# Two transformer layers on one core: set-up, sum and order rewritten, and Q's parts, V's bias and the normalisation shared among three engines

## The chip, the cores and the metric

One core of a Trainium2 chip runs the whole program. Its engines are TensorE (PE, with its weight loads shown apart as PEld), VectorE (DVE), ScalarE (ACT), GpSimd (POOL) and SyncE (SP, which only issues DMAs here). Each runs its own instructions strictly in the order of the program, and they meet at semaphores. The metric is the device time of one execution in microseconds (us).

## The reference

`x` is 2 batches x 512 rows x 128. Two layers follow each other.

```
layer 0:  w = softmax over the batch axis of (cond . x) / sqrt(128);  h = x * w
          x = x + down(silu(gate(h)) * up(h))       gate, up: 128 -> 512, down: 512 -> 128
          (inputs rounded to 8 bits by row, weights to -1, 0, 1)
layer 1a: causal attention, 16 heads of 8, with one image key and value ahead of the 512 words
layer 1b: y = c_proj(attention) ;  full attention, 16 heads of 8, on y ;  out_proj
          x3 = layernorm(y + attention(y))
          moe: 4 groups x 2 experts, 128 -> 256 -> 128, one expert chosen for each row
          x = x + layernorm(x3 + moe(x3))
```

## The kernel before

**Instances.** The attention is computed four times: instances a = 0 and 1 are the causal attention of batch 0 and 1, a = 2 and 3 the full attention of batch 0 and 1. An instance needs Q, K and V (steps `q`, `k`, `v`). Q and K are each split into three bf16 parts that add up to the fp32 value: part 1 by ACT (`Qp[:, 0]`), the rest `qres` and parts 2 and 3 by DVE (lines 936 to 939 for Q, 943 to 946 for K). The parts go to DRAM and come back stacked, nine rows for each of the 8 dimensions of a head, into `Qs` and `Ks` [128, 2, 16, 512] (SP's step `v`, lines 489 to 507). Rows 64 and up of these stacks have to be zero or hold fixed values (shift, mask) before that; POOL zeroes them with memsets of 64x4096 fp32 words (lines 564, 565, 573, 574), and SP writes the fixed rows (lines 468 to 473).

**Scores twice.** For each head and each tile of 128 rows, PE computes the scores (line 1232) and DVE reduces them to a row maximum (step `scores`: line 968 for the causal instances, 972 for the full ones), 64 steps an instance. The maxima, negated (`max`), are transposed (`max_rows`) and sent by SP into two rows of `Qs`. Then PE computes the scores again, transposed and shifted by the maximum (`attend`, line 1255, 32 steps an instance), ACT takes the exponential (line 751) and PE multiplies with V (`values`, line 1273; four rounds of four heads, the result in `ps_pv`). ACT copies it out, PE turns it (`turn_back`), and DVE normalises: it adds the image's share from `Zimg` (line 1003, causal instances only), takes the reciprocal of the denominator (1007) and multiplies (1008). `V` gets its bias from DVE on its way out of `ps_misc` (line 953).

**Sum, norm and experts.** Step `sum` computes c_proj's and out_proj's results into `ps_misc`, twelve matmuls after `o_rows` of the batch's second instance:

```
for t in range(NT):
    o = ps[:, t * D:(t + 1) * D]
    pe.matmul(o, OT[:, a, t * P:(t + 1) * P], Wcp[:, :], start=True, stop=False)
    pe.matmul(o, OT[:, 2 + a, t * P:(t + 1) * P], WsqT[:, 0, :], start=False, stop=False)
    mm = pe.matmul(o, ones[0:1, :], brow[:, 2, :], start=False, stop=True)
```

On DVE the same step is the whole layer norm (lines 791 to 809), with POOL's power between its halves (line 620). Then come router and combine weights, and for each of 8 experts `hidden` (PE line 1342 into `ps_s0` and `ps_s1`; DVE and ACT take the relu) and `y` (PE line 1350 into `ps_misc`; DVE adds it to `acc`, line 1074). Step `out` is the last norm, again in one piece.

**Order.** `MERGE` is a string of 576 letters. Each letter names a chain (of `f` and `g`, the first layer and Q, K, V of batch 0 and 1; `0` to `3`, scores; `A` to `D`, attend; `a` to `d`, values and turning back; and others), and takes its next step. The result, `ORDER`, is gone through by every engine, which issues what it has to do in each step. So where DVE's part of a step stands among DVE's work, and PE's among PE's, comes from the one string. `ps_misc` is one bank that most small jobs pass through one after another, and scores have two banks (`ps_s0`, `ps_s1`), or four where no attend is near. The first layer's buffers and those of the later steps lie in one region, `shared`.

## Time and profile before

| | us |
|---|---|
| median of 3 runs | 382.31 (380.33 to 384.16) |
| the profiled execution | 381.2 |
| its span, first to last instruction | 379.4 |
| PE busy | 307.3 (81%) |
| DVE busy | 261.2 (69%) |
| ACT busy | 171.2 (45%) |
| POOL busy | 42.5 (11%) |

The profiled execution took 1.8 us more than its span. Busy time of PE counts a matmul from its start to its modelled end, and matmuls overlap, so a busy PE need not be at its peak. An operation's share of the time of a stage is read from the start of one to the start of the next.

### The profile page before, as it was taken

The numbers are of one execution on the slowest core, as the hardware profiler recorded it, in microseconds if no ns is written. First come the engines' busy times: TensorE is split into PE (matmuls) and PEld (weight loads), VectorE is DVE, ScalarE is ACT, GpSimd is POOL, SyncE is SP. The second block draws the span as 40 slices with busy tenths as digits, with TensorE's granted clock in tenths as the row PEclk, the third lists the DMA queues.
The fourth block names the chain that finished last, engine by engine and source line by source line (L and its number), as shares of the span: only waits on it lengthen the run. The fifth ranks groups of instructions, "written<-read, shape, count | busy, mean of one in ns | idle before, by whom it ended". The sixth has DMA issues, their size and how long they took to land.

```text
span 379.4 us, 5450 instructions
## 1 busy us (share of the span) xinstructions
PE 307.3 (81%) x1900; PEld 153.9 (41%) x1900; DVE 261.2 (69%) x763; ACT 171.2 (45%) x246; POOL 42.5 (11%) x56
## 2 busy tenths in 40 slices
PE   0251985897898999868999989999999987987980
PEld 0120733253453644433433222343434455655760
DVE  3979457997786887869989878877721135557444
ACT  2664134005455657443678565665777511220210
POOL 9189500000000000000000000002000001001001
PEclk9996566558999999999999999999999999999997
DMA  6101307601670004710006700160000000000001
GB/s 184 46 2 18 46 0 214 146 1 50 177 141 1 3 4 148 184 41 2 2 14 189 168 4 0 29 196 2 2 2 0 0 2 0 3 0 28 2 0 29
DMA packets 14719, 19.69 MB, mean 52 GB/s; under 512 B 2142, under 2 KB 12258, under 8 KB 14116
## 3 DMA queue, kind: packets, MB, share of 16 engines
q1 hardware_dynamic: 14404, 19.06, 19.3%
q0 software_dynamic: 288, 0.28, 0.6%
q8 instruction: 15, 0.25, 0.3%
q14 instruction: 12, 0.10, 0.1%
HBM read 13.99 MB, written 4.72 MB: 49 GB/s over the span
## 4 chain that ended last, share of the span: by engine, by line
PE 48%; DVE 24%; issue 14%; DMA 6%; ACT 5%; POOL 1%; SPq 1%; POOLq 0%; DVEq 0%; ACTq 0%
PE ps_pv L1273 11%; DVE mx L972 8%; PE ps_s L1232 8%; PE ps_t L1255 7%; DMA Qs<-nmT 5%; PE ps_s L1342 4%; PE ps_misc L1350 3%; PE ps_misc L1208 2%; DVE shared L968 1%; DVE shared L809 1%; DVE probs L902 1%; DMA X<-in_x 1%; ACT probs L751 1%; PE ps_misc L1238 1%; DVE mx L968 1%
## 5 line engine op out<-in xcount | busy, mean ns | idle before, releaser
L751 ACT ACTIVATE probs<-ps_t 128x1024 f32<-128x1024 f32 (+2 forms) x128 | 106.6, 862 | 62.9 <-PE ps_t L1258 33.9
L972 DVE TENSOR_REDUCE mx<-ps_s 128x1 f32<-128x512 f32 x128 | 82.0, 686 | 14.2 <-PE ps_s L1232 14.0
L1232 PE MATMUL ps_s<-Ks,Qs 128*128 128x512 bf16 (+3 forms) x237 | 78.0, 353 | 9.5 <-DVE mx L972 3.0
L1255 PE MATMUL ps_t<-Qs,Ks 128*128 128x512 bf16 (+3 forms) x256 | 67.9, 340 | 5.2 <-DMA Qs<-nmT 5.1
L1273 PE MATMUL ps_pv<-probs,Vs 128*32 128x512 f32 (+3 forms) x512 | 57.2, 524 | 0.4 <-ACT probs L751 0.2
L968 DVE CUSTOM_DVE_ANT_0 shared<-ps_s,shared 128x256 bf16<-128x256 f32 (+3 forms) x109 | 47.3, 465 | 10.9 <-PE ps_s L1232 10.3
L1232 PEld LDWEIGHTS ps_s<-Ks,Qs 128*128 128x128 bf16 x237 | 22.4, 99 | 65.5 <-DVE mx L972 30.8
L1074 DVE SCALAR_TENSOR_TENSOR shared<-ps_misc,comb,shared 128x128 f32<-128x128 f32 x64 | 18.1, 344 | 31.3 <-PE ps_misc L1350 31.1
L1350 PE MATMUL ps_misc<-Ks,shared 128*128 128x128 f32 x256 | 31.6, 277 | 5.5 <-DVE shared L1074 2.4
L1255 PEld LDWEIGHTS ps_t<-Qs,Ks 128*128 128x128 bf16 x256 | 23.5, 98 | 30.9 <-issue 8.0
L1350 PEld LDWEIGHTS ps_misc<-Ks,shared 128*128 128x128 f32 x256 | 30.5, 192 | 11.9 <-issue 11.5
L737 ACT ACTIVATE shared<-ps_s,cols 128x512 f32<-128x512 f32 x16 | 11.0, 688 | 47.3 <-PE ps_s L1342 47.3
L1342 PE MATMUL ps_s<-Qf,Ks 128*128 128x512 f32 x64 | 30.4, 598 | 0.8 <-DVE shared L1065 0.8
L620 POOL TENSOR_TENSOR rstd<-ve,halves 128x4 f32<-128x4 f32 x4 | 4.2, 1039 | 210.1 <-DVE ve L797 210.1
L1258 PE MATMUL ps_t<-causal_k,identb 128*128 128x128 bf16 x128 | 24.5, 219 | 0.0
L1273 PEld LDWEIGHTS ps_pv<-probs,Vs 128*32 128x32 f32 x512 | 10.7, 108 | 19.5 <-issue 17.8
L1065 DVE TENSOR_SCALAR shared<-ps_s,cols 128x512 f32<-128x512 f32 x16 | 11.9, 745 | 8.0 <-PE ps_s L1342 8.0
L614 POOL TENSOR_TENSOR Zimg<-Vimg,Pimg 128x288 f32<-128x288 f32 x4 | 2.7, 682 | 111.7 <-ACT Pimg L731 95.7
L1342 PEld LDWEIGHTS ps_s<-Qf,Ks 128*128 128x128 f32 x64 | 11.0, 190 | 9.8 <-issue 8.5
L734 ACT ACTIVATE shared<-ps_pv 128x512 f32<-128x512 f32 x16 | 9.5, 594 | 11.7 <-PE ps_pv L1273 11.7
L1258 PEld LDWEIGHTS ps_t<-causal_k,identb 128*128 128x128 bf16 x128 | 12.5, 98 | 3.9 <-issue 0.3
L714 ACT ACTIVATE Qf<-ps_misc,cols 128x512 f32<-128x512 f32 x2 | 1.4, 688 | 23.5 <-PE ps_misc L1208 23.5
(240 smaller groups left out, 361.9 us busy)
## 6 DMA issues: line engine op xcount, KB each, us to landing
parts_q<-Qp SPq DMA_DIRECT2D x20, 128.0 KB, 2.0
Qs<-parts_q SPq DMA_DIRECT2D x24, 96.0 KB
Ks<-parts_k SPq DMA_DIRECT2D x24, 96.0 KB
Qs<-parts_q SPq DMA_DIRECT2D x12, 192.0 KB
Ks<-parts_k SPq DMA_DIRECT2D x12, 192.0 KB
parts_k<-Kp SPq DMA_DIRECT2D x12, 128.0 KB, 1.8
Ks<-in_L_ffn_w SPq DMA_DIRECT2D x1, 1024.0 KB, 5.8
X<-in_x SPq DMA_DIRECT2D x2, 256.0 KB, 4.4
```

What stands on the lines that cost most here:

```text
L737: act.activation(hid[:, i % 2, 1, :], ps[:, :], ACT.Relu, bias=cols17[:, 2 * i + 1:2 * i + 2])\
L751: act.activation(probs[:, half % 2, j, 0:w], ps[:, 0:w], ACT.Exp).then_inc(free[f"t{i % 2}"], 1)
L968: last = dve.tensor_tensor_reduce(out=added[:, n % 2, 0:w], in0=ps[:, 0:w], in1=causal_q[:, S - w:], scale=1.0, scalar=LEAST, op0=ALU.add, ...
L972: last = dve.tensor_reduce(mx[:, b, t, h:h + 1], ps[:, 0:w], AX, ALU.max)
L1065: dve.tensor_scalar(hid[:, i % 2, 0, :], ps[:, :], cols17[:, 2 * i:2 * i + 1], 0.0, ALU.add, ALU.max).then_inc(free["s0"], 1)
L1074: last = dve.scalar_tensor_tensor(out=acc[:, a, t, :], in0=ps[:, t * D:(t + 1) * D], scalar=comb[:, a, t, i // 2, i % 2:i % 2 + 1], in1=ac ...
L1232: mm = pe.matmul(ps[:, 0:w], Qs[:, b, h, t * P:(t + 1) * P], Ks[:, b, h, 0:w], start=True, stop=True)
L1255: mm = pe.matmul(ps[:, col:col + w], Ks[:, b, h, kb * P:(kb + 1) * P], Qs[:, b, h, S - w:S], start=True, stop=(a >= 2))
L1258: mm = pe.matmul(ps[:, col:col + P], identb[:, :], causal_k[:, :], start=False, stop=True)
L1273: mm = pe.matmul(ps[j * HC:(j + 1) * HC, S - w:S], Vs[:, b, kb, r * GROUP + j, :], probs[:, half % 2, j, col:col + w], start=(kb == 0), st ...
L1342: pe.matmul(ps[:, :], W1[:, i, h * P:(h + 1) * P], X3T[:, a, :], start=True, stop=True)\
L1350: mm = pe.matmul(ps[:, t * D:(t + 1) * D], hid[:, i % 2, h, t * P:(t + 1) * P], W2[:, i, h, :], start=(h == 0), stop=(h == FH - 1))
```

## The change

1. **Zeroing.** DVE zeroes rows 64 and up of `Qs` of batch 0 as its first instruction, and SP copies that megabyte three times, by DMA, to `Ks` of batch 0, `Qs` of batch 1 and `Ks` of batch 1 (behind its 17 loads of weights). The fixed rows and the first two stacks wait for all three copies. POOL keeps only the memsets of `Vs`, and its nine small loads move to the middle of instance 2.
2. **Steps cut into smaller ones.** A step that several engines shared at one place of the order has now one letter for each part: `x1`, `round_x`, `images`, `fixed_rows`, `q_parts`, `k_parts`, `send`, `keep`, `image`, `relu`, `add`, `routed`, and the norm as `centre` and `spread`, with statistics, `ve` and `rstd` kept apart for each of the four norms. `X3` and `combT` have one place for each batch.
3. **Sum.** The bias (one matmul of 512 columns) and c_proj's four matmuls form `presum`, which can stand ahead of `o_rows`; only out_proj's four remain in `sum`. Batch 1's sum is in `ps_pv`.
4. **Other engines.** ACT casts Q's part 2 and POOL subtracts for part 3 (`q_mid`). ACT copies V out of PSUM and POOL adds its bias in SBUF (`v_bias`). In rounds 0 to 2 of each instance ACT copies the turned sums to `sums`, POOL adds the image's share (causal instances), DVE takes the reciprocal and POOL multiplies (`normalise`, `shares`). Round 3 stays on DVE. K's parts stay on DVE.
5. **The string** has 697 letters in another order.

The core of the diff, in the order SP, POOL, ACT, DVE, PE:

```diff
+                    sp.wait_ge(rows_first, 1)
+                    for stack in (Ks[HALF_ROWS:, 0, :, :], Qs[HALF_ROWS:, 1, :, :], Ks[HALF_ROWS:, 1, :, :]):
+                        sp.dma_start(stack, Qs[HALF_ROWS:, 0, :, :]).then_inc(rows_zeroed, 16)
-                if step == "prepare":
+                if step == "fixed_rows":
...
                     sp.wait_ge(pool_const, 1)
                     sp.wait_ge(mparts_ready, 1)
+                    sp.wait_ge(rows_zeroed, 16 * 3)
```

```diff
+                if step == "q_mid":
+                    pool.wait_ge(qrest_ready, a * (PARTS - 1) + 1)
+                    pool.tensor_tensor(Qp[:, 2, :], qres[:, :], Qp[:, 1, :], ALU.subtract).then_inc(qrest_ready, 1)
+                if step == "v_bias":
...
+                    pool.wait_ge(free["misc"], filled("misc", "v", a))
+                    bias = vbias[:, a // 2, :].rearrange("p (h d) -> p h d", d=HD)
+                    pool.tensor_tensor(Vs[:, b, :, :, 0:HD], Vs[:, b, :, :, 0:HD],
+                                       bias.unsqueeze(1).to_broadcast([P, NT, HEADS, HD]), ALU.add)\
+                        .then_inc(v_ready, 1)
+                if step == "normalise" and a < 2 and i < ROUNDS - 1:
...
+                    pool.tensor_tensor(sums[:, :, :, :], sums[:, :, :, :], Zimg[:, b, :, heads, :], ALU.add)\
+                        .then_inc(round_sum, 1)
+                if step == "shares":
+                    heads = slice(i * GROUP, (i + 1) * GROUP)
+                    pool.wait_ge(rden_ready, a * (ROUNDS - 1) + i + 1)
+                    pool.tensor_tensor(On[:, :, heads, :], sums[:, :, :, 0:HD],
+                                       rden[:, :, :].unsqueeze(3).to_broadcast([P, NT, GROUP, HD]), ALU.mult)\
+                        .then_inc(turned_ready, 1)
```

```diff
+                if step == "q_mid":
+                    act.wait_ge(qres_ready, a + 1)
+                    act.activation(Qp[:, 1, :], qres[:, :], ACT.Copy).then_inc(qrest_ready, 1)
...
+                if step == "normalise" and i < ROUNDS - 1:
+                    if a * ROUNDS + i > 0:
+
+                        act.wait_ge(turned_ready, turned(a, i))
+                    tb = take("misc", "turn_back", a, i)[:, :].rearrange("p (t j c) -> p t j c", j=GROUP, c=HC)
+                    act.activation(sums[:, :, :, :], tb[:, :, :, 0:HD + 1], ACT.Copy).then_inc(free["misc"], 1)
```

```diff
+            def centre(n, src, dst, gain):
 
                 for t in range(NT):
+                    last = dve.bn_stats(stats[:, n, t, :], src[:, t, :])
                 then_wait(last)
                 for t in range(NT):
+                    last = dve.bn_aggr(mv[:, n, t, :], stats[:, n, t, :])
                 then_wait(last)
+                dve.tensor_scalar(ve[:, n, :], mv[:, n, :, 1], EPS, None, ALU.add).then_inc(ve_ready[n], 1)
                 for t in range(NT):
+                    read = dve.scalar_tensor_tensor(out=dst[:, t, :], in0=src[:, t, :], scalar=mv[:, n, t, 0:1],
                                                     in1=norm_gb[:, gain, :], op0=ALU.subtract, op1=ALU.mult)
+                return read
+
+            def spread(n, dst, more):
+
+                dve.wait_ge(rstd_ready[n], 1)
                 for t in range(NT):
+                    last = dve.scalar_tensor_tensor(out=dst[:, t, :], in0=dst[:, t, :], scalar=rstd[:, n, t:t + 1],
                                                     in1=more(t), op0=ALU.mult, op1=ALU.add)
                 return last
...
+                    dve.memset(Qs[HALF_ROWS:, 0, :, :].rearrange("p h s -> p (h s)").bitcast(fp32), 0.0)\
+                       .then_inc(rows_first, 1)
```

```diff
+                if step == "presum":
...
+                    ps = put(SUM_AT[a], "sum", a)
+                    pe.matmul(ps[:, :].rearrange("p (t d) -> p t d", d=D), ones[0:1, :],
+                              brow[:, 2:3, :].to_broadcast([1, NT, D]), start=True, stop=False)
+                    for t in range(NT):
+                        pe.matmul(ps[:, t * D:(t + 1) * D], OT[:, a, t * P:(t + 1) * P], Wcp[:, :],
+                                  start=False, stop=False)
```

Of the string two stretches, before and after, each from the end of batch 0's first layer to the first scores:

```
-  ggffffffffwfgffggggggggg000000
+  gf!4Ugggggggg00000v00000000000
```

Three places in the order of the instructions. **DVE, from the first layer's `down` of batch 0 to Q's rest.** `Vimg`, `vbias` and `bjoin` are the image's values and the joined biases, `X<-ps_pv` is x1 (its four rows of 128 in one row), `probs<-probs,ps_t` with `q<-probs` is one `ffn_up` of batch 1. Before:

```order
L882 TENSOR_SCALAR kimg<-ps_misc,cols 128x2
L886 TENSOR_SCALAR Kimg<-head_of,kimg 128x16 x2
L891 COPY Vimg<-ps_s 128x16x8 x2
L893 COPY vbias<-ps_s 128x128
L895 TENSOR_SCALAR bjoin<-ps_s,cols 128x1 x2
L929 SCALAR_TENSOR_TENSOR X<-ps_pv,q,X 128x128 x4
L902 TENSOR_TENSOR probs<-probs,ps_t 128x512
L905 TENSOR_REDUCE q<-probs 128x1
```

Now:

```order
L988 COPY R2T<-ps_t 128x512 x2
L995 SCALAR_TENSOR_TENSOR X<-ps_pv,q,X 128x128 x4
L968 TENSOR_TENSOR probs<-probs,ps_t 128x512
L971 TENSOR_REDUCE q<-probs 128x1
L968 TENSOR_TENSOR probs<-probs,ps_t 128x512
L971 TENSOR_REDUCE q<-probs 128x1
L968 TENSOR_TENSOR probs<-probs,ps_t 128x512
L971 TENSOR_REDUCE q<-probs 128x1
L1002 TENSOR_TENSOR qres<-Qf,Qp 128x512
L968 TENSOR_TENSOR probs<-probs,ps_t 128x512
```

x1 of batch 0 follows `down` at once; three of batch 1's four `ffn_up` and all of the image's work moved behind it.

**DVE, a round of instance 0 that is normalised among the scores of instance 1** (`shared,mx<-ps_s` and `mx` are one score step). Before:

```order
L968 ISA shared,mx<-ps_s,shared 128x128
L968 ISA mx 128x1
L1003 TENSOR_TENSOR sums<-ps_misc,Zimg 128x144
L1007 RECIPROCAL rden<-sums 128x16
L1008 TENSOR_TENSOR shared<-sums,rden 128x4x32
L968 ISA shared,mx<-ps_s,shared 128x256
L968 ISA mx 128x1
```

Now:

```order
L1021 ISA mx 128x1
L1054 RECIPROCAL rden<-sums 128x16
L1021 ISA shared,mx<-ps_s,shared 128x384
L1021 ISA mx 128x1
L1021 ISA shared,mx<-ps_s,shared 128x512
```

Of three instructions one stays, at a place of its own.

**PE, where batch 1's attention ends and its sum begins** (`ps_s<-Qf,Ks` is `hidden`, `ps_misc<-Ks,shared` is `y`). Before:

```order
L1273 MATMUL ps_pv<-probs,Vs 32x512 x8
L1284 MATMUL ps_misc<-ident,shared 128x128 x4
L1292 MATMUL ps_misc<-ident,shared 128x128 x4
L1342 MATMUL ps_s<-Qf,Ks 128x512 x2
L1302 MATMUL ps_misc<-Wcp,shared 128x128
L1303 MATMUL ps_misc<-WsqT,shared 128x128
L1304 MATMUL ps_misc<-brow,ones 128x128
```

Now:

```order
L1336 MATMUL ps_pv<-probs,Vs 32x512 x16
L1418 MATMUL ps_misc<-Ks,shared 128x128 x8
L1362 MATMUL ps_pv<-brow,ones 128x512
L1365 MATMUL ps_pv<-Wcp,shared 128x128 x4
L1347 MATMUL ps_misc<-ident,shared 128x128 x4
L1410 MATMUL ps_s<-Qf,Ks 128x512 x2
L1354 MATMUL ps_misc<-ident,shared 128x128 x4
L1418 MATMUL ps_misc<-Ks,shared 128x128 x8
L1371 MATMUL ps_pv<-WsqT,shared 128x128 x4
L1410 MATMUL ps_s<-Qf,Ks 128x512 x2
```

Bias and c_proj went ahead of `o_rows`; between `o_rows` and the norm stand one `y` and four matmuls.

## Rows read from the trace of the kernel before

**Rows 1.** Busy time in seven stretches: bounds, length, PE, PEld, DVE, ACT, POOL, PEclk, DMA share, GB/s

```profile
6.43:66.35 59.92, 30.96 (x146) 18.10 (x146) 44.75 (x110) 25.59 (x50) 27.55 (x24) 0.74 0.25 63
66.35:102.80 36.45, 31.31 (x141) 13.84 (x140) 31.81 (x136) 10.33 (x16) 0.68 (x1) 0.72 0.33 89
102.80:155.60 52.80, 48.10 (x412) 25.80 (x412) 40.33 (x168) 30.81 (x49) 1.37 (x2) 1.00 0.30 72
155.60:270.80 115.20, 106.77 (x669) 40.94 (x668) 95.67 (x180) 69.99 (x89) 2.98 (x3) 1.00 0.25 62
270.80:304.40 33.60, 31.64 (x206) 13.35 (x205) 8.84 (x35) 21.64 (x26) 0.00 (x0) 1.00 0.00 1
304.40:370.60 66.20, 58.51 (x332) 41.85 (x332) 35.07 (x116) 11.55 (x18) 3.32 (x3) 1.00 0.02 5
370.60:379.40 8.80, 0.01 (x1) 0.00 (x0) 4.72 (x21) 0.00 (x0) 1.04 (x1) 0.76 0.11 31
```

**Rows 2.** Timeline of DVE, set-up: start, us, line, operation, [idle before <-releaser]

```profile
9.02 2.21 DVE L824 TENSOR_SCALAR wdot<-wdot 128x8 f32<-128x8 f32 x1
...
29.11 3.32 DVE L913 TENSOR_SCALAR q<-q,wmean 128x4 f32<-128x4 f32 x1
...
36.51 2.04 DVE L919 TENSOR_SCALAR shared<-probs 128x512 bf16<-128x512 f32 x2
...
48.53 0.49 DVE L891 COPY Vimg<-ps_s 128x128 f32<-128x128 f32 x2 [4.03 <-PE ps_s L1148]
...
49.38 1.12 DVE L929 SCALAR_TENSOR_TENSOR X<-ps_pv,q,X 128x128 f32<-128x128 f32 x4
53.35 0.69 DVE L902 TENSOR_TENSOR probs<-probs,ps_t 128x512 f32<-128x512 f32 x1 [2.85 <-ACT probs L691]
...
59.14 0.69 DVE L946 TENSOR_TENSOR Kp<-kres,Kp 128x512 bf16<-128x512 f32 x1
...
66.35 0.29 DVE L968 CUSTOM_DVE_ANT_0 shared<-ps_s,shared 128x128 bf16<-128x128 f32 x1 [0.81 <-PE ps_s L1232]
```

**Rows 3.** Timeline of POOL, set-up

```profile
7.69 3.51 POOL L565 MEMSET Ks<- 64x4096 f32 x1
...
28.89 3.51 POOL L573 MEMSET Qs<- 64x4096 f32 x1
```

**Rows 4.** The DMA queue of SP, set-up: start and time of the issue

```profile
11.12 0.25 SPq L458 DMA_DIRECT2D brow<-in_L_ffn_out_proj_b  x1
...
35.99 1.85 SPq L468 DMA_DIRECT2D Ks<-shared  x3
...
56.04 2.47 SPq L489 DMA_DIRECT2D parts_q<-Qp  x5
```

**Rows 5.** DMA issues by size: KB each, us from issue to landing

```profile
Ks<-in_L_ffn_w SPq DMA_DIRECT2D x1, 1024.0 KB, 5.8
```

**Rows 6.** Groups by line of DVE: count, busy us, mean ns, idle before

```profile
L939 DVE TENSOR_TENSOR Qp<-qres,Qp 128x512 bf16<-128x512 f32 x4 | 2.8, 692 | 0.1
...
L953 DVE TENSOR_TENSOR Vs<-ps_misc,vbias 128x512 f32<-128x512 f32 x4 | 2.7, 687 | 0.3 <-PE ps_misc L1217 0.3
L1003 DVE TENSOR_TENSOR sums<-ps_misc,Zimg 128x144 f32<-128x144 f32 x8 | 2.4, 301 | 0.0
L1008 DVE TENSOR_TENSOR shared<-sums,rden 128x128 f32<-128x128 f32 x8 | 2.3, 292 | 0.3
...
L937 DVE CAST Qp<-qres 128x512 bf16<-128x512 f32 x4 | 1.7, 427 | 0.1
```

**Rows 7.** Groups by line of POOL

```profile
L625 POOL TENSOR_TENSOR X<-X,norm_gb 128x512 f32<-128x512 f32 x2 | 2.5, 1270 | 0.0
```

**Rows 8.** Timeline of DVE at two hand-offs of the attention and at batch 1's sum

```profile
145.13 0.69 DVE L936 TENSOR_TENSOR qres<-Qf,Qp 128x512 f32<-128x512 f32 x1 [2.22 <-ACT Qp L717]
...
258.45 0.89 DVE L791 BATCH_NORM_STATS2 stats<-ps_misc 128x6 f32<-128x128 f32 x4 [3.02 <-PE ps_misc L1304]
...
310.87 0.89 DVE L791 BATCH_NORM_STATS2 stats<-ps_misc 128x6 f32<-128x128 f32 x4 [4.20 <-PE ps_misc L1304]
```

More of the change, by code:

```diff
@@ L85, in program_order @@
         "l": [("load_experts", 0, 0)],
-        "n": route(0),
-        "s": route(1),
-        "e": each("hidden", 0, EXPERTS) + each("hidden", 1, EXPERTS),
-        "y": each("y", 0, EXPERTS) + each("y", 1, EXPERTS),
-        "o": [("out", 0, 0)],
-        "p": [("out", 1, 0)],
+        "e": both("hidden", EXPERTS),
+        "x": both("relu", EXPERTS),
+        "y": both("y", EXPERTS),
+        "z": both("add", EXPERTS),
     }
@@ L94, in program_order @@
         chains["0123"[a]] = each("scores", a, HEADS * NT)
+        chains["4567"[a]] = [(n, a, 0) for n in ("q_parts", "k_parts", "send")]
+        chains["EFGH"[a]] = [("v_bias", a, 0)]
         chains["ABCD"[a]] = each("attend", a, UNITS)
         chains["abcd"[a]] = output(a)
+        chains["MNOP"[a]] = each("keep", a, ROUNDS)
+        chains["IJKL"[a]] = each("normalise", a, ROUNDS)
+        chains["WXYZ"[a]] = each("shares", a, ROUNDS - 1)
+        chains["!#$%"[a]] = [("q_mid", a, 0)]
+    for b in range(B):
+        chains["ns"[b]] = [(n, b, 0) for n in ("presum", "sum", "x3t", "router", "combine", "bias2")]
+        chains["QR"[b]] = [(n, b, 0) for n in ("centre", "spread", "routed", "route", "acc0")]
+        chains["op"[b]] = [("centre", b, 1), ("spread", b, 1), ("out", b, 0)]
     taken = {name: iter(steps) for name, steps in chains.items()}
@@ L146, in place_jobs @@
         if step in ("x1t", "q", "k", "v", "o_rows",
-                    "sum", "x3t", "router", "combine", "bias2"):
+                    "x3t", "router", "combine", "bias2"):
             add("misc", step, a)
+        if step == "presum":
+            add(SUM_AT[a], "sum", a)
         if step == "scores":
             add(where[a, i], "scores", a, i)
-        if step == "max" and a < 2:
+        if step == "image":
             add("misc", "image", a, i)
@@ L418, in three_parts, with turned @@
                            ap=[[HEADS * S, PARTS * HD], [1, (hi - lo) * S]])
+        def turned(a, i):
+            return sum(ROUNDS if n < 2 else ROUNDS - 1 for n in range(a)) + i
         block = ctx.enter_context(nc.Block())
@@ L778, in take, with rounded_x @@
                 return place[n]
+            def rounded_x(n):
+                tiles = slice(n * NT, (n + 1) * NT)
+                for t in range(n * NT, (n + 1) * NT):
+                    last = dve.tensor_scalar(xtmp[:, t, :], X[:, t, :], wdot[:, 0, t:t + 1], q1[:, 1, t:t + 1],
+                                             ALU.mult, ALU.mult)
+                then_wait(last)
+                dve.tensor_scalar(R1[:, tiles, :], xtmp[:, tiles, :], MAGIC, MAGIC, ALU.add, ALU.subtract)\
+                   .then_inc(r1_ready, 1)
             def ternary(n):
@@ L992, in _ @@
                            .then_inc(simg_ready, 1)
-                if step == "turn_back":
+                if step == "shares":
+                    if a < 2:
+                        dve.wait_ge(round_sum, a * (ROUNDS - 1) + i + 1)
+                    else:
+                        dve.wait_ge(free["misc"], filled("misc", "turn_back", a, i))
+                    if a * ROUNDS + i > 0:
+                        dve.wait_ge(turned_ready, turned(a, i))
+                    dve.reciprocal(rden[:, :, :], sums[:, :, :, HD]).then_inc(rden_ready, 1)
+                if step == "normalise" and i == ROUNDS - 1:
+                    dve.wait_ge(turned_ready, turned(a, i))
                     ps = take("misc", "turn_back", a, i)
@@ L1234, in _ @@
                     mm.then_inc(full[SCORES[a, i]], 1)
[L1235 removed]
+                if step == "image":
                     ps = put("misc", "image", a, i)
```

231 lines of the change are left out of this document (111 added, 120 removed).

## Prediction

> **What bounds the kernel now.** I read the windows first [rows 1]. They cut the span where the work changes: set-up and first layer up to the first score at 66.35 us, causal scores up to 155.6, full scores up to 270.8, the last attends with the first experts up to 304.4, the experts, and a tail of 8.8 us. Until 66.35 no engine is full (of 59.9 us DVE has 44.8, PE 31.0), so a chain through all engines sets the time. From there to 102.8 DVE is busy 31.8 of 36.5 us while PE's granted clock is 0.72, between its two levels of 1.2 and 2.4 GHz; DVE sets the pace. In the causal scores after that PE shows 48.1 and DVE 40.3 of 52.8, in the full ones 106.8 and 95.7 of 115.2: two engines that feed each other through a few PSUM banks, each near its limit. From 270.8 on PE does almost everything (31.6 of 33.6, then 58.5 of 66.2 us) and DVE matters only where PE waits for it.
>
> Next comes DVE's timeline of the set-up beside POOL's [rows 2, 3]. An operation on 128x8 elements takes 2.21 us and ends at 11.23; POOL's memset of `Ks` ends at 7.69 + 3.51 = 11.20. One on 128x4 takes 3.32 us and ends at 32.43; the memset of `Qs` ends at 32.40. The two that follow them into the next batch of work (36.51, 2.04 us for a pair) are slow in the same way. So the memsets hold DVE up, not only POOL. The reader also sees DVE wait 4.03 us for the image's V and 2.85 us for a silu, both between `down` of batch 0 and its Q.
>
> **The change, part by part.** All sums are in us saved against the profiled execution, 381.2 (span 379.4 and 1.8 around it).
>
> *Set-up.* The first short operation loses its wait, but what follows needs the weights' sums from ACT and PE, which POOL does not hold up: I take 1.2 of the possible 2.0. The second loses 3.1. The pair loses about 1.0: two at 0.43, as for the cast of line 937 [rows 6], would be 0.9, and V's memsets stay and may hit it. The image's work stood ahead of x1 of batch 0: 4.03 of waiting and 0.85 of DVE (48.53 to 49.38), 4.9. The wait of 2.85 goes too, since three `ffn_up` of batch 1 now fill the time in which PE and ACT make Q. Q's parts 2 and 3 leave DVE's chain to K's parts: 0.43 + 0.69 [rows 6], 1.1. That is 14.1. Against it, the image's 0.9 still comes ahead of the first score, with perhaps 1.0 of waiting for PE. The first score then stands near 66.3 - 12.2 = 54. But x1 of batch 1, 1.1 [rows 2], now falls behind the first scores, so **11** are saved. Ends: 6, if the image's work, for which DVE now waits 4.03 [rows 2], delays batch 1's `down` by as much and 1 us is lost around it, and 14, if nothing new waits.
>
> DVE's memset of 64x4096 appears in no row. DVE's rows give 0.43 us for 512 elements of a partition at best and 0.69 at worst [rows 6], so 3.4 to 5.5 us for 4096. It starts with the program and DVE's first work waits for `x` until 6.43, where the first window begins. I take it as hidden; without that cover it would cost its excess over about 5.5, at most a few tenths. The three copies follow SP's last load, 11.37 [rows 4]. A megabyte from DRAM landed in 5.8 us [rows 5], so three take some 17 and land near 29. The twelve fixed-row DMAs at 0.62 each [rows 4] end at 37, and Q's first part is ready at about 40 to 42 (before, 56.04 [rows 4]). Cost nothing, but with few us to spare; this is a rival below.
>
> *Causal scores, 66.35 to 155.60.* DVE loses Q's parts of two instances (2.2), V's bias of three (3 x 0.69 = 2.1) and, in three rounds, the add and the product (3 x (0.30 + 0.29) = 1.8) [rows 6]: 6.1, or some 5.5 start to start. The 2.22 us that DVE stood for Q of instance 2 [rows 8] can be filled, since `q_parts` is now some scores behind `q`. Sum 7.7. PE was at 48.1 of 52.8 in the larger part, so not all comes through: **6**, between 0 (PE or the order takes it all) and 12 (the new order also fills part of the 17 us in which DVE idles here [rows 1]).
>
> *Full scores, 155.60 to 270.80.* DVE loses 1.1 and 0.7 for instance 3, and in rounds 0 to 2 of instances 1 and 2 1.8 and 0.9: 4.5. The sum of batch 0 kept DVE waiting 3.02 us [rows 8]; 8 of its 12 matmuls now come before, so about 2.0 goes. Sum 6.5; with PE at 106.8 of 115.2 I take **5**, between 1 and 10.
>
> *Last part, 270.80 on.* Batch 1's sum made DVE wait 4.20 us [rows 8], two thirds of it or 2.8 go. In the experts PE idles 66.2 - 58.5 = 7.7 us, mostly while DVE does a whole norm between two relus. `centre` and `spread` let relus and adds between: I give 2.2 of what is left. **5**, between 1 and 9. The tail of 8.8 stays: the last norm has nothing beside it.
>
> *What is added.* ACT gets a cast, a copy and three small copies an instance, some 3 us of ACT an instance by its neighbours on DVE; it was busy 70 of 115 in the full scores. POOL gets Q's part 3 and V's bias, 1.27 each by a POOL row of the same shape [rows 7] (0.7, as on DVE, to 1.3), and the shares, all on an engine that is nearly idle there. Queued behind ACT's new waits are exponentials; behind PE's wait for `v_ready` come `values`, but the bias is many scores ahead of them. I cost them at nothing; the bound is the last rival. POOL's nine loads move behind shares of instance 1, and their data are first needed at the norm of batch 0, tens of us later.
>
> Sum: 11 + 6 + 5 + 5 = 27. 381.2 - 27 = 354.2; the median lies 1.1 above the profiled execution, so **355**.
>
> **The rivals.** *The copies are late.* No row shows a copy within SBUF of this size. Were they half as fast as row 5 says, they would land at 46, the fixed rows would go out until 54, and Q's and K's parts only then: scores at 63. They decide from a landing at about 34 on, a us for a us. The set-up would give 2 instead of 11: 364.
>
> *Attention gives nothing.* PE's 93% in the full scores is its limit, or the two scores' banks are, and what DVE is spared becomes waiting for PE. For it: PE's share. Against: its busy time counts overlapping matmuls. 11 + 5 = 16 saved, 366.
>
> *A lock between POOL and DVE.* The rows above show DVE held to the end of a memset. POOL's new 1.27 us for Q's part 3 falls beside K's rest on DVE, in each instance: 4 x 1.27 = 5 us, and 360. The Trainium skill says so in general, on its page SBUF — State Buffer, section Who interferes with whom: DVE and GpSimd share a port pair that one instruction holds to its end, and a DVE instruction with two SBUF inputs collides with a GpSimd one that reads SBUF. By that rule V's bias and the shares do no harm, since scores read PSUM; the two long short operations agree with it.
>
> *Slower.* Every round now goes PE, ACT, POOL, DVE, POOL where it went PE, DVE, and Q's parts DVE, ACT, POOL. In an in-order ACT the copy that frees `ps_misc` stands between exponentials; if PE comes late with `turn_back`, ACT waits, the exponentials behind it are late, and PE's next attends with them. There are 12 rounds, 4 Q and 4 V, 20 hand-offs. The gain is gone when each costs the bound engine 1.35 us, and at 1.55 the kernel is 1% slower; a hand-off of Q cost DVE 2.22 before. At 1.9 it is 38 - 27 = 11 slower: 392. Against it: `Ou` has two buffers, and DVE and PE have scores between.
>
> **How the numbers follow.** Forecast 0.54; copies late 0.13; attention gives nothing 0.13; lock 0.09; two or more of these together so that it ends within 1% 0.05; slower 0.06. One per cent, 3.8 us, is about what a measurement of this kernel can tell from no change (its three runs span 3.8). Faster: 0.89, same 0.05, slower 0.06. All the low ends at once give 373, all the high ones 336; neither is likely. The range 341 to 371 holds the first four cases.
>
> **What would show it.** In the trace after: the first score near 54; no short DVE operation of over 1 us in the set-up; three copies landed before 34; the end of the scores near 249; DVE's wait for batch 1's sum about 1.4; some 103 or 104 us from the last score to the end where it was 108.6. Wrong would be: PE at the low clock beyond the first attends (its granted clock was 1.00 from 102.8 up to the tail [rows 1]), ACT waiting over a us at the copies of `sums`, or the fixed rows behind the copies.

## The result, and the profile after

| | before | after |
|---|---|---|
| median | 381.3 us (380.2 to 384.2, 4 runs) | 362.0 us (361.7 to 364.2, 4 runs) |
| profiled execution, span | 381.2, 379.4 | 361.8, 359.9 |

The ratio is 0.950 (95% interval 0.943 to 0.956). Forecast were 355 us and 27 saved; the spans of the profiled executions differ by 19.5. Some executions, of whatever version, take some per cent longer than the others of the same kernel; they are left out of what is compared below.

**Where it was saved.** The windows of the changed kernel, with the columns of [rows 1]. The causal scores run from 53.31 to 143.18, the full ones to 257.09:

```profile
1.66:53.31 51.65, 25.83 (x141) 15.98 (x142) 40.80 (x105) 26.43 (x51) 14.23 (x31) 0.93 0.64 148
53.31:89.76 36.45, 29.14 (x160) 14.80 (x164) 34.19 (x146) 12.55 (x20) 4.78 (x4) 0.81 0.39 98
89.76:143.18 53.42, 46.64 (x400) 24.50 (x405) 34.98 (x150) 33.10 (x55) 6.50 (x10) 0.94 0.28 66
143.18:257.09 113.91, 103.65 (x635) 39.72 (x648) 90.14 (x163) 68.72 (x93) 14.51 (x23) 0.97 0.28 65
257.09:290.00 32.91, 32.10 (x207) 14.76 (x203) 7.29 (x31) 23.75 (x32) 0.81 (x2) 1.00 0.00 1
290.00:352.01 62.01, 56.07 (x330) 40.79 (x329) 35.51 (x123) 10.62 (x17) 3.69 (x4) 1.00 0.02 5
352.01:359.90 7.89, 0.00 (x1) 0.00 (x0) 4.72 (x21) 0.00 (x0) 1.04 (x1) 0.69 0.11 33
```

| stage | before | after | saved | forecast |
|---|---|---|---|---|
| up to the first score | 66.35 | 53.31 | 13.0 | 12.2 |
| causal scores (x1 of batch 1 now in them, -1.1) | 89.3 | 89.9 | -0.5 | 6 - 1.1 |
| full scores | 115.1 | 113.9 | 1.2 | 5 |
| from the last score to the end | 108.6 | 102.8 | 5.8 | 5 |

Set-up and last part gave what was forecast. The attention (the two rows of scores) gave 0.7 instead of 9.9, although DVE was spared nearly what it should be: from the first to the last score it was busy 159.3 us where it had 167.8 in [rows 1]. The reader should see two things in the windows: PE too is busy less than before, and its granted clock, 1.00 from 102.8 on before, is 0.94 and 0.97 here.

**The set-up.** DVE's timeline, to be held against [rows 2]:

```profile
1.66 3.47 DVE L889 MEMSET Qs<- 64x4096 f32 x1 [1.66 <-PEq L1439]
6.55 1.29 DVE L894 TENSOR_TENSOR shared<-X,shared 128x512 f32<-128x512 f32 x2 [1.42 <-DMA X<-in_x]
...
9.13 0.17 DVE L899 TENSOR_SCALAR wdot<-wdot 128x8 f32<-128x8 f32 x1
...
25.82 0.85 DVE L977 TENSOR_SCALAR q<-q 128x4 f32<-128x4 f32 x1
...
26.91 0.24 DVE L979 TENSOR_SCALAR q<-q,wmean 128x4 f32<-128x4 f32 x1
...
34.69 1.13 DVE L995 SCALAR_TENSOR_TENSOR X<-ps_pv,q,X 128x128 f32<-128x128 f32 x4 [0.49 <-PE ps_pv L1247]
...
45.09 0.69 DVE L1009 TENSOR_TENSOR Kp<-kres,Kp 128x512 bf16<-128x512 f32 x1
...
53.31 0.29 DVE L1021 CUSTOM_DVE_ANT_0 shared<-ps_s,shared 128x128 bf16<-128x128 f32 x1 [2.81 <-PE ps_s L1293]
```

The memset took 3.47 us and ended 1.42 before `x` was there. The operations of 2.21 and 3.32 us now take 0.17 and 0.24. What is left of the effect are three short ones of 0.6 to 0.85 us: two, at 25.82 and 27.05, beside an addition for a bias and the smaller memsets of `Vs` on POOL, and one at 42.89 (0.84 where the same operation took 0.24 at 26.91) beside Q's part 3, which the change gave to POOL. x1 of batch 0 stands 14.7 us earlier. SP's queue in the same stretch, against [rows 4]:

```profile
12.82 2.68 SPq L492 DMA_DIRECT2D Ks<-Qs  x1
29.63 1.85 SPq L502 DMA_DIRECT2D Ks<-shared  x3
...
33.92 4.27 SPq L502 DMA_DIRECT2D Ks<-shared  x3
...
40.56 4.65 SPq L525 DMA_DIRECT2D parts_q<-Qp  x5
```

The three copies landed 7.1, 11.9 and 16.7 us after their issue, the last at 29.5; the fixed rows went out from there until 40.5.

**The attention.** PE's timeline shows three stops at the first attend of the second eight heads, in instances 0, 1 and 2. Before and now:

```profile
115.83 0.39 PE L1255 MATMUL ps_t<-Qs,Ks 128*128 128x512 bf16 x1 [1.18 <-DMA Qs<-nmT]
...
165.57 0.39 PE L1255 MATMUL ps_t<-Qs,Ks 128*128 128x512 bf16 x1 [2.70 <-DMA Qs<-nmT]
...
220.15 0.60 PE L1255 MATMUL ps_t<-Qs,Ks 128*128 128x512 bf16 x2 [1.25 <-DMA Qs<-nmT]
```

```profile
100.76 0.61 PE L1316 MATMUL ps_t<-Qs,Ks 128*128 128x512 bf16 x1 [4.83 <-DMA Qs<-nmT]
...
153.27 0.39 PE L1316 MATMUL ps_t<-Qs,Ks 128*128 128x512 bf16 x1 [2.88 <-DMA Qs<-nmT]
...
208.67 1.03 PE L1316 MATMUL ps_t<-Qs,Ks 128*128 128x512 bf16 x2 [2.12 <-DMA Qs<-nmT]
```

The chain that ended last, around the first stop (start, us, what):

```profile
91.29 0.47 ACT nmT L778
91.76 0.02 issue
91.78 0.65 SPq L548
92.43 0.04 issue
92.47 8.24 DMA Qs<-nmT
...
100.76 0.61 PE ps_t L1316
```

`nmT` are the negated maxima, 8 KB a DMA, and the second takes 8.24 us to land. SP issued instance 1's stack copies (18 DMAs, 2.3 MB) until 90.8, 1.0 us ahead of the rows; before, 3.3 us lay between the two:

```profile
104.36 1.18 SPq L507 DMA_DIRECT2D Ks<-parts_k  x3
108.88 1.33 SPq L512 DMA_DIRECT2D Qs<-nmT  x2
```

The rows came 9 to 10 us after the last stack copy had been issued, before and now: PE went on 10.3, 8.8 and 9.3 us after it before, and 10.0, 8.8 and 10.2 now, although the rows were issued from 0.04 to 5.4 us behind it. So the sooner PE gets there, the longer it stops. For the second eight heads of instance 0 PE was there 9.1 us after the last stack copy before and is there after 5.1 now; in instances 1 and 2 that hardly moved (6.1 to 6.0, and 8.1 both times), and the stops there grew by 0.2 and 0.9 only. What follows the first stop is in the windows:

```profile
96.00:100.00 4.00, 0.00 (x0) 0.00 (x0) 0.55 (x4) 0.40 (x1) 0.27 (x1) 0.87 0.58 104
100.00:104.00 4.00, 3.24 (x14) 0.83 (x14) 0.43 (x2) 0.00 (x0) 0.00 (x0) 0.50 0.00 0
104.00:108.00 4.00, 4.00 (x29) 1.29 (x29) 2.00 (x9) 1.54 (x2) 0.41 (x1) 0.78 0.00 0
```

PE is at the low level of its clock (0.50, 1.2 GHz) until 105.8, and again from 153.6 to 157.0 and from 208.2 to 211.6. From the restart that is 5.0, 3.4 and 2.9 us at half speed, a loss of 5.7 if PE set the pace throughout. The stops grew by 9.8 - 5.1 = 4.7. Together 10.4, and 9.2 were missing (9.9 forecast with x1 of batch 1 counted in, 0.7 found). An account that comes out nearly even is no proof yet.

### The profile page after: what moved, and what is told of

Same layout as the page of the kernel before. It is cut to its first block, busy times and chain, and to the rows that moved or that the text cites. A ratio compares the mean times of both kernels' runs of the same rounds, so it can differ in the third digit from the quotient of the medians.

```text
span 359.9 us, 5454 instructions
## 1 busy us (share of the span) xinstructions
PE 293.4 (82%) x1861; PEld 150.5 (42%) x1888; DVE 247.7 (69%) x734; ACT 176.1 (49%) x266; POOL 46.5 (13%) x84
## 4 chain that ended last, share of the span: by engine, by line
PE 48%; DVE 18%; issue 16%; DMA 8%; ACT 5%; SPq 3%; POOLq 0%; POOL 0%; DVEq 0%; another core or an unknown queue 0%; ACTq 0%
PE ps_pv L1336 13%; PE ps_t L1316 10%; PE ps_s L1293 8%; DMA Qs<-nmT 6%; PE ps_misc L1418 4%; DVE mx L1025 4%; PE ps_s L1410 4%; ACT probs L803 2%; DVE shared L1021 2%; DVE probs L968 2%; DMA shared<-in_L_ffn_w_down 2%; DVE mx L1021 1%; PE ps_t L1319 1%; DVE q L971 1%; SPq L543 1%
## 5 line engine op out<-in xcount | busy, mean ns | idle before, releaser
L803 ACT ACTIVATE probs<-ps_t 128x1024 f32<-128x1024 f32 (+2 forms) x128 | 105.8, 862 | 57.7 <-PE ps_t L1319 26.6
L1293 PE MATMUL ps_s<-Ks,Qs 128*128 128x512 bf16 (+3 forms) x218 | 70.4, 354 | 9.9 <-DVE mx L1021 3.3
L1336 PE MATMUL ps_pv<-probs,Vs 128*32 128x512 f32 (+3 forms) x512 | 58.3, 536 | 0.7 <-DVE mx L1025 0.3
L1316 PEld LDWEIGHTS ps_t<-Qs,Ks 128*128 128x128 bf16 x256 | 24.2, 99 | 35.3 <-DMA Qs<-nmT 11.4
L657 POOL TENSOR_TENSOR shared<-sums,rden 128x128 f32<-128x128 f32 x12 | 4.9, 407 | 123.5 <-DVE rden L1054 123.5
L1336 PEld LDWEIGHTS ps_pv<-probs,Vs 128*32 128x32 f32 x512 | 11.0, 109 | 21.0 <-issue 19.3
L672 POOL TENSOR_TENSOR shared<-shared,halves 128x4 f32<-128x4 f32 x4 | 4.1, 1035 | 70.3 <-DVE shared L872 70.3
L1021 DVE CUSTOM_DVE_ANT_0 shared<-ps_t,shared 128x512 bf16<-128x512 f32 (+1 forms) x21 | 12.5, 623 | 0.3 <-remote 0.2
## 6 DMA issues: line engine op xcount, KB each, us to landing
Ks<-Qs SPq DMA_DIRECT2D x2, 1024.0 KB, 11.9
Qs<-Qs SPq DMA_DIRECT2D x1, 1024.0 KB, 11.9
```

What stands on the lines that cost most here:

```text
L803: act.activation(probs[:, half % 2, j, 0:w], ps[:, 0:w], ACT.Exp).then_inc(free[f"t{i % 2}"], 1)
L1021: last = dve.tensor_tensor_reduce(out=added[:, n % 2, 0:w], in0=ps[:, 0:w], in1=causal_q[:, S - w:], scale=1.0, scalar=LEAST, op0=ALU.add, ...
L1293: mm = pe.matmul(ps[:, 0:w], Qs[:, b, h, t * P:(t + 1) * P], Ks[:, b, h, 0:w], start=True, stop=True)
L1316: mm = pe.matmul(ps[:, col:col + w], Ks[:, b, h, kb * P:(kb + 1) * P], Qs[:, b, h, S - w:S], start=True, stop=(a >= 2))
L1336: mm = pe.matmul(ps[j * HC:(j + 1) * HC, S - w:S], Vs[:, b, kb, r * GROUP + j, :], probs[:, half % 2, j, col:col + w], start=(kb == 0), st ...
```

## The experiments

The kernels ran in three groups of four, each on a chip of its own, with runs of the kernel before beside them (medians 379.8, 380.7 and 380.2). Ratios are to those. A version of the changed kernel that an edit neither helps nor slows should stay at 362.0, ratio 0.950. "Less" and "more" are differences of medians, often across groups, and 1 us of them means nothing.

### Who holds the shift rows up

**shift_pool:**

```diff
-                if step == "max_rows":
...
-                        sp.dma_start(Qs[SHIFT + n:SHIFT + n + 1, b, i * HALF:(i + 1) * HALF, :],
...
+                if step == "max_rows":
...
+                        pool.dma_start(Qs[SHIFT + n:SHIFT + n + 1, b, i * HALF:(i + 1) * HALF, :],
```

> Edit: the two DMAs that write the shift rows of a half (Qs<-nmT) go out from GpSimd's queue instead of SyncE's; all else is as in the changed kernel (362.0 us, causal scores 89.9 us, full scores 113.9 us from first to last). Theory Q (the rows of the second half stand in SyncE's queue behind the next instance's eighteen stack copies; PE stops 4.8, 2.9 and 2.1 us, and its granted clock is then 0.5 for 5.0, 3.2 and 3.3 us): the rows land in 2 to 4 us instead of 8.2, 8.0 and 4.1, the three stops fall to under 2 us each, the clock stays at 1.00, and the time is 350 to 355. Rival E (the transfer engines are full of stack copies whichever queue asks, so the rows land as late as before): stops and clock as they are, 361 to 363. Rival P (PE or DVE are the limit and what a stop gives back is lost elsewhere): the stops go, and the time is still 360 or more.

Measured: 360.1 us (357.4 to 362.7), ratio 0.948 [0.938, 0.958]: not to be told from the changed kernel. The median hides two pairs, 357.4 and 357.6 us, and 362.6 and 362.7; the profile is of the 362.6, and what made the other two shorter is not known. Its timeline of GpSimd and of PE:

```profile
94.95 1.08 POOL L658 DMA_DIRECT2D Qs<-nmT  x2 [10.48 <-ACT nmT L778]
...
103.14 0.61 PE L1316 MATMUL ps_t<-Qs,Ks 128*128 128x512 bf16 x1 [4.09 <-DMA Qs<-nmT]
```

Of the 16 DMAs the median landed in 1.9 us and the slowest in 8.2; the stops were 4.09, 3.09 and 1.69, and the rows landed 9.1, 9.0 and 9.7 us after the last stack copy was issued, as they did from SP's queue. So in the run that was profiled it is not the place in SP's queue: rival E holds there, and what counts are the bytes in front. That another queue never helps is not shown by one profile.

**split_send:**

```diff
                 if step == "send":
                     for g, (lo, hi) in enumerate(RANGES):
+                        if g == 2 and a > 0:
+                            continue
                 if step == "max_rows":
...
+                    if i == 1 and a < 3:
+                        dram_q, dram_k = parts_dram[a + 1]
+                        lo, hi = RANGES[2]
...
+                            sp.dma_start(Qs[r:r + PARTS * HD, 1 - b, lo:hi, :].rearrange("p h s -> p (h s)"),
+                                         three_parts(dram_q[n], lo, hi)).then_inc(stacked_q[a + 1][2], 16)
```

> Edit: for instances 1 to 3 the third range of the stack copies (heads 8 to 15, six DMAs, half of the bytes) goes out of SyncE's queue behind the shift rows of the instance before instead of ahead of them. Theory Q: only half of the bytes are still in front, the rows of the second half land in 4 to 6 us instead of 8.2 and 8.0, the stops of PE (4.8, 2.9, 2.1) fall to 0 to 2 us, and the low clock behind them goes with them: 352 to 357. Rival E': the rows take 8 us because of their own shape (16 KB each into a row of one partition), not because of what is in front: 361 to 363. Cost if the late third range now holds the scores of heads 8 on: a stop at the thirty-third score of each instance, at most a us or two, since that score is over 15 us away.

Measured: **348.1 us** (347.1 to 350.1), ratio 0.918 [0.910, 0.926], 14 less than the changed kernel and below the expected range. Of the wait for `nmT` 1.1 us in all is left, on two weight loads, and the late range stops nobody. SP's queue and the windows of the scores:

```profile
87.05 1.18 SPq L545 DMA_DIRECT2D Ks<-parts_k  x3
91.67 1.34 SPq L550 DMA_DIRECT2D Qs<-nmT  x2
93.05 1.28 SPq L557 DMA_DIRECT2D Qs<-parts_q  x3
```

```profile
90.00:136.00 46.00, 44.76 (x403) 23.91 (x401) 34.80 (x148) 32.56 (x55) 6.49 (x10) 1.00 0.29 73
136.00:190.00 54.00, 51.36 (x354) 21.15 (x352) 47.88 (x85) 33.40 (x52) 11.26 (x19) 1.00 0.35 77
190.00:242.00 52.00, 50.95 (x293) 17.80 (x291) 42.02 (x80) 34.97 (x42) 3.30 (x5) 1.00 0.25 65
```

The clock is 1.00 throughout and PE is busy 97, 95 and 98%. The causal scores take 82.4 us and the full ones 106.1: 6.9 and 9.0 less than before the change. Rival E' falls with it, for the rows have the same shape as ever.

**warm:**

```diff
-                    if i % (UNITS // 2) == 0:
-                        pe.wait_ge(shifted[a][i // (UNITS // 2)], 16 * 2)
...
                     ps = put(f"t{i % 2}", "weights", a, i)
+                    if i == UNITS // 2 and a < 3:
+                        for _ in range((22, 13, 9)[a]):
+                            pe.matmul(ps[:, 0:S], identb[:, :], Ks[:, b, 0, :], start=True, stop=True)
+                    if i % (UNITS // 2) == 0:
+                        pe.wait_ge(shifted[a][i // (UNITS // 2)], 16 * 2)
```

> Edit: in front of the wait for the second half's shift rows, PE does 22, 13 and 9 matmuls of 512 columns in instances 0, 1 and 2 whose result is overwritten (about 4.7, 2.8 and 1.9 us, as long as the three stops). The wait itself stays. Theory C (the stop costs twice: the wait itself, and then a granted clock of 0.5 for 5.0, 3.2 and 3.3 us, of which half or 5.8 us is lost): the clock stays at 1.00 there and the time falls by 4 to 6, to 356 to 358. Rival (the low clock behind the stops costs nothing, because DVE's reductions or the rows' data set the pace there): 361 to 364.

Measured: 359.1 us (357.0 to 360.8), ratio 0.945 [0.937, 0.952], 2.9 less than the changed kernel. The windows of the first stop, filled, and behind it:

```profile
100.00:102.00 2.00, 2.00 (x11) 0.93 (x10) 0.00 (x0) 0.00 (x0) 0.00 (x0) 1.00 0.00 0
102.00:104.00 2.00, 2.00 (x17) 0.72 (x15) 0.43 (x2) 0.00 (x0) 0.00 (x0) 1.00 0.00 0
```

The clock stays at 1.00 at all three places. The full scores, with two of the stops, are 2.4 us shorter, where 6.3 us at half speed had been; the causal scores only 0.6, and in them the clock fell twice more, for 3.4 us each, from 70.4 and from 84.1, where the changed kernel's had stayed at 1.00 from 68.3. So the low clock behind a stop costs time of its own, as the full scores show. Of the 4 to 6 expected some 3 came, and the intervals of the two kernels overlap; against the 14 of split_send the waits themselves are the larger part.

**before_split:** the same edit as in split_send, in the kernel before.

> Edit: the kernel before, with the third range of the stack copies of instances 1 to 3 behind the shift rows of the instance before, and nothing else changed. In its trace PE waits 1.18, 2.70 and 1.25 us for the second half's rows, and its granted clock stays at 1.00. Theory Q (the rows' place in the transfers is what costs): it gains those waits and DVE's waits behind them (1.50, 2.87, 1.38), 4 to 6 us: 375 to 377 against 380 to 381; much less than the 14 of the changed kernel, because there the new order had put the rows right behind the copies and the clock fell. Rival O (the late third range helps the scores in some other way, not by the stops): it gains as much as in the changed kernel, 10 or more, 371 or less.

Measured: 374.2 us (372.6 to 374.8), ratio 0.981 [0.976, 0.985], 6.4 less than the 380.7 beside it (7.4 by the ratio): just below theory Q's range and short of rival O's. PE no longer stops. It is more than the 5.1 us of stops and half of the 14 of the changed kernel. The collision was there all along; the change doubled its price.

With the range late in both kernels, the stages tell what the change itself is worth. The causal and the full scores of before_split (no clock is recorded in it before 87.3, which the view counts as 1.00):

```profile
67.77:153.83 86.06, 76.92 (x543) 39.34 (x553) 72.06 (x304) 40.75 (x65) 2.05 (x3) 1.00 0.31 81
153.83:264.64 110.81, 104.10 (x656) 41.01 (x668) 95.62 (x181) 70.24 (x89) 2.98 (x3) 1.00 0.26 65
```

From there to split_send the first score comes 13.9 us earlier, the causal scores take 3.6 less (82.4), the full ones 4.7 less (106.1), and the rest 5.5 less (108.3 to 102.8): 27.7 in the two profiles. By the medians, from two chips, it is 26.1, and by the two ratios 24.

### What the parts of the change are worth

**all_dve** (in the changed kernel) and **split_all_dve** (in split_send's): the rounds of instances 0 to 2, and Q's parts and V's bias of all four, return to DVE.

```diff
                 if step == "q_parts":
...
+                    dve.tensor_copy(Qp[:, 1, :], qres[:, :]).then_inc(qrest_ready, 1)
+                    dve.wait_ge(qrest_ready, a * (PARTS - 1) + 1)
+                    dve.tensor_tensor(Qp[:, 2, :], qres[:, :], Qp[:, 1, :], ALU.subtract).then_inc(qrest_ready, 1)
+                if step == "v_bias":
...
+                    dve.tensor_tensor(Vs[:, b, :, :, 0:HD],
...
-                if step == "normalise" and i == ROUNDS - 1:
+                if step == ("turn_back" if a < 3 else "normalise") and (a < 3 or i == ROUNDS - 1):
```

> Edit: Q's parts 2 and 3, V's bias and rounds 0 to 2 of the normalisation of instances 0 to 2 are done by DVE again, at the steps where DVE or ACT has them; the string, the zeroing, the set-up and the sum stay as changed, and so do the rounds of instance 3. DVE gets back 4 x 1.1 for Q, 4 x 0.69 for V and 6 x 0.59 + 3 x 0.29 for the rounds, 11.6 us in all. Theory W (the attention is bound by PE's stops, DVE has slack between them): the time moves by 3 at most, 359 to 366. Rival D (DVE's busy time in the attention is what sets the pace, so the offload is worth what it takes off DVE, and the stops hide it in the total only): 370 to 374.

Measured: 365.3 us (364.3 to 366.4), ratio 0.961 [0.955, 0.968], 3.3 more, in theory W's range.

> Edit: the version with the late third range (348.1 us, PE without a stop of over 1 us in the attention) and in it Q's parts 2 and 3, V's bias and rounds 0 to 2 of the normalisation of instances 0 to 2 back on DVE. DVE's busy time grows by 8.1 us, as it did in the changed kernel (247.7 to 255.8), where the time grew by 3.3. Theory W2 (while PE stood still at the shift rows, DVE caught up, so its extra work was partly covered; without the stops it counts in full): 355 to 357, that is 7 to 9 more. Rival L (PE's own work is the limit and DVE's slack is the same as with the stops): 350 to 352, 2 to 4 more.

Measured: 357.3 us (356.7 to 360.0), ratio 0.939 [0.934, 0.944], 9.1 more than split_send; against split_fixed, which ran on the same chip, 9.6. Both theories W hold by their numbers: the offload is worth some 9 us where PE does not stop, and 3 where it does. That DVE caught up during the stops is argued and not shown, and part of the difference may be the clock's: in all_dve's profile it fell with the first two stops only (4.25 and 3.03 us, and not with one of 2.65), for 6.8 us after the restarts instead of 11.4, and once more for 3.4 us in the first scores.

**split_n_dve** and **split_q_dve** return the rounds alone and Q's parts alone:

> Edit: the version with the late third range, with rounds 0 to 2 of the normalisation of instances 0 to 2 back on DVE and Q's parts and V's bias left to ScalarE and GpSimd. All three together cost 9.1 us. DVE gets back 6 x 0.59 + 3 x 0.29 = 4.4 us. Theory M (each part of the offload is worth what it takes off DVE): 352 to 353. Rival V (the normalisation is worth more than its busy time, since DVE also has to wait for turn_back there and the scores behind it are late): 354 or more. Rival R (it is worth nothing, since DVE does these beside PE's attends): 349 or less.

Measured: 353.2 us (352.3 to 353.8), ratio 0.928 [0.925, 0.931], 5.1 more, for 4.4 us of work.

> Edit: the version with the late third range, with Q's parts 2 and 3 back on DVE and the rest left as it is. DVE gets back 4 x (0.43 + 0.69) = 4.5 us, and GpSimd no longer does 1.16 us beside K's rest on DVE. Theory M: 351 to 353. Rival K (GpSimd's subtraction slows K's rest on DVE by as much as it spares, and the parts are ready later, so the offload of Q is worth nothing): 347 to 349.

Measured: 349.1 us (347.9 to 351.6), ratio 0.918 [0.914, 0.923], 0.9 more, which cannot be told from nothing, for 4.5 us of work: rival K. In the profiles DVE is busy only 2.4 us more (250.0 against 247.6), since operations that POOL's subtraction had slowed are back at their own length. V's bias is left with some 3 of the 9.1, by subtraction; no run returned it alone. The changed kernel's timelines show the slowing, POOL first:

```profile
78.40 1.16 POOL L637 TENSOR_TENSOR Qp<-qres,Qp 128x512 bf16<-128x512 f32 x1 [1.91 <-ACT Qp L806]
79.52 1.73 POOL L645 TENSOR_TENSOR Vs<-Vs,vbias 128x512 f32<-128x512 f32 x1
```

```profile
78.88 1.23 DVE L1006 TENSOR_TENSOR kres<-Kf,Kp 128x512 f32<-128x512 f32 x1
80.14 1.39 DVE L1007 CAST Kp<-kres 128x512 bf16<-128x512 f32 x1
...
188.87 0.68 DVE L1006 TENSOR_TENSOR kres<-Kf,Kp 128x512 f32<-128x512 f32 x1
189.59 0.43 DVE L1007 CAST Kp<-kres 128x512 bf16<-128x512 f32 x1
...
197.72 1.00 DVE L1036 TENSOR_SCALAR nm<-mx 128x32 bf16<-128x32 f32 x1
```

Beside POOL's two operations K's rest takes 1.23 and 1.39 us, elsewhere 0.68 and 0.43: 1.5 us. At 197.72 V's bias of instance 3 (POOL, 197.40 to 198.68) lies beside an operation that takes 0.18 elsewhere: 0.8. With the 0.6 at 42.89 that is 3.0 us at three places.

**zero_pool** and **split_zero_pool** return the zeroing to POOL:

```diff
-                        sp.dma_start(stack, Qs[HALF_ROWS:, 0, :, :]).then_inc(rows_zeroed, 16)
...
+                    for stack in (Qs, Ks):
+                        pool.memset(stack[HALF_ROWS:, a, :, :].rearrange("p h s -> p (h s)").bitcast(fp32), 0.0)\
...
-                    dve.memset(Qs[HALF_ROWS:, 0, :, :].rearrange("p h s -> p (h s)").bitcast(fp32), 0.0)\
```

> Edit: the changed kernel with the zeroing of rows 64 and up of the four stacks back in GpSimd's memsets (3.51 us each, two after each memset of Vs) and neither DVE's memset nor the three copies. By the terms of the prediction DVE is held up by 1.2 + 3.1 + 1.0 = 5.3 us more: first score at about 58.5 instead of 53.3, time 366 to 368. Rival N (what set the first score after the change is the chain of SyncE's DMAs, fixed rows, parts and stacks, which has several us of cover for DVE): first score at 53 to 55 and 361 to 363.

Measured: 364.0 us (363.6 to 365.7 in three of the four runs; the fourth took 389.6), ratio 0.956 [0.951, 0.961], 2.0 more (2.8 by the median of all four, as the next expectation has it): between the two theories. The profile is of the fourth run and is not compared.

> Edit: the version with the late third range (348.1 us), with the zeroing of rows 64 and up back in GpSimd's memsets, and neither DVE's memset nor the three copies. Theory D (the memsets hold DVE up by about the forecast's 5.3 us, the first score moves from 53.8 to 59 or 60, and with no stop at the shift rows the whole of it comes through to the end): 353 to 355. Rival G (a later first score is made good in the causal scores, as it was in the changed kernel, which lost only 2.8 us by this edit): 350 to 351.

Measured: 355.9 us (354.6 to 356.3), ratio 0.935 [0.932, 0.938], 7.7 more; first score at 60.9. POOL's timeline and DVE's:

```profile
29.09 3.51 POOL L617 MEMSET Qs<- 64x4096 f32 x1
32.66 3.70 POOL L617 MEMSET Ks<- 64x4096 f32 x1
```

```profile
30.92 5.73 DVE L998 TENSOR_SCALAR shared<-probs 128x512 bf16<-128x512 f32 x2
```

Two casts that take 0.76 together in the changed kernel take 5.73. Theory D holds, at 7 instead of 5.3, and the time is 0.9 above its range. Why the same edit costs only 2 us where the stops are is open.

**split_one_sum:**

```diff
-                if step == "presum":
...
+                if step == "sum":
...
+                        pe.matmul(o, OT[:, a, t * P:(t + 1) * P], Wcp[:, :], start=True, stop=False)
+                        pe.matmul(o, OT[:, 2 + a, t * P:(t + 1) * P], WsqT[:, 0, :], start=False, stop=False)
+                        mm = pe.matmul(o, ones[0:1, :], brow[:, 2, :], start=False, stop=True)
```

> Edit: the version with the late third range, with all twelve matmuls of a sum together at step sum, as in the kernel before, and nothing at presum. Theory F (the forecast's terms: 2.0 us for batch 0's sum, which stands among the full scores, and 2.8 for batch 1's, which stands in the last part): 351 to 353, and DVE waits for batch 1's sum. Rival X (a y and a hidden stand between o_rows and the sum now, so that the matmuls are done on PE either way and DVE has adds to do; only the matmuls' own excess, twelve for nine with the loads, counts): 348 to 350.

Measured: 354.3 us (351.3 to 355.0), ratio 0.929 [0.925, 0.933], 6.1 more. In the profiles the full scores are 2.2 and the last part 3.0 us longer, the two terms 2.0 and 2.8 of the forecast. The causal scores, which the edit does not touch, are 2.8 us longer too, and in them PE's clock came back at 76 us instead of 68. One of the two waits of [rows 8] is back, that of batch 0; before batch 1's norm DVE still does not wait:

```profile
239.05 0.89 DVE L880 BATCH_NORM_STATS2 shared<-ps_misc 128x6 f32<-128x128 f32 x4 [3.38 <-PE ps_misc L1378]
```

**split_fixed:**

```diff
                 if step == "fixed_rows":
-                    for b in range(B):
+                    for b in [0]:
...
+                if step == "send" and a == 0:
+                    for c in [1]:
+                        for n in range(PARTS):
```

> Edit: the version with the late third range, and the six fixed-row DMAs of batch 1 (6.8 us of SyncE's time, 33.9 to 40.5) behind instance 0's stack copies instead of ahead of its parts. Theory S (Q's first part is ready before 40 and SyncE gets to it only at 40.56, so the queue is the limit of the first score): first score 1 to 3 us earlier, 345 to 347. Rival K (K's part 3, ready at 45.8, sets the stacks and with them the first score): first score within 0.5 us of 53.8 and the time within 1 of 348.

Measured: 347.7 us (347.3 to 348.1), ratio 0.912 [0.909, 0.915]. The first score came at 51.6, 2.2 us earlier, as theory S has it, but the time moved by 0.4, as rival K has it. In this profile PE's clock came back at 75 us, in split_send's at 68, so the two cannot be compared by stage. It is the fastest version, by less than can be told.

## Why the prediction was right or wrong

The sign and the range were right. The saving forecast was 7 to 8 us too large (27 against 19.3 by the medians), and the shortfall is in one place: the attention gave 9.2 less than forecast, set-up and last part 1.6 more. The range caught it; 362.0 lies nearer to the numbers of two rivals that did not happen as told (360 and 364) than to 355.

- *Set-up, 12.2 earlier.* 13.0 were found. The copies were to land near 29 and landed at 29.5; Q's parts went out at 40.56; the fixed rows ended at 40.5, not 37, because batch 1's three took 4.27 us. The memsets were worth 7.0 at the first score (60.9 against 53.8 in split_send) rather than 5.3, and all the rest 6.0 rather than 6.9: DVE now waits 2.81 us for the first score where it had 0.81, because SP's chain of fixed rows and parts ends last. The memset hidden behind `x`: 3.47 us, right.
- *Causal scores 6, full scores 5.* This is the step that failed. The sizes were not far off: with the third range late in both kernels the two stages save 3.6 + 4.7 = 8.3 us, where 9.9 were forecast with x1 in them, and the whole change 24 to 28, where 27 were. What was wrong is "I cost them at nothing" for what is added or moved. I looked at ACT, at POOL and at PE's wait for `v_ready`, but not at SP: `send` and `max_rows` are both in its queue. The shift rows land 9 to 10 us after the stack copies in front of them are issued, and in the new order PE wants those of instance 0 after 5.1 us instead of 9.1. The stops grew by 4.7 us, and a low clock behind them, which was not there before, cost some more. [rows 1] could not show it; PE's three waits for `nmT` and the place of the stack copies were in the trace before. Why the third stop grew by 0.9 is open.
- *Last part 5, tail unchanged.* 5.8; 3.0 of it is batch 1's sum (split_one_sum), and 0.9 lies in the tail, which I had left out: the last DMA lands 2.3 us after its issue instead of 3.2, and nothing in the change bears on that. DVE does not wait for batch 1's sum at all, where 1.4 was forecast; a relu ends just ahead of it. 102.8 us lie between last score and end, where 103 or 104 were forecast.
- *Rivals.* Copies late: no. Attention gives nothing: its number was nearly right for the two stages (0.7, or 1.8 without x1, instead of 11) and its reason wrong, since without the stops they gave 7.4 and 7.8 us more. The lock: 3.0 us at three places instead of 5 at four; POOL's part 3 met K's rest in one instance only. I had held V's bias to be harmless, and half of the 1.5 us there and the 0.8 at 197.72 are beside it. The Trainium skill, page SBUF — State Buffer, section Who interferes with whom, counts casts with two-port modes among what a GpSimd operation can block; the cast that went from 0.43 to 1.39 agrees. Slower by hand-offs: ACT waited 1.21 us at most at the copies of `sums` (once, for POOL's product); without the stops the offload earned its 9 us.
- *The signs.* "PE at the low clock beyond the first attends" was named as one that would make it wrong, and that is what the trace shows; so was ACT waiting over a us at the copies of `sums`, which it did once. The end of the scores, forecast near 249, came at 257.1. The first score, the short operations of the set-up and the landing of the copies are as forecast.

## What to carry to other kernels

Of a step that moves, follow its DMAs too: a small transfer that an engine waits for should not stand behind megabytes that nobody needs yet. Here moving the bytes helped and another queue did not. A stop of PE can be paid twice, once as the wait and once at the low clock behind it. What an offload is worth can be read only after the stops are gone (3 us with them, 9 without), so mend the largest wait before judging the rest. And a collision that both kernels have is best taken out of both: then the change gave about what its parts add up to (24 to 28 us, 27 forecast).
